# Attention B: projections of tiles 2 to 5 issued earlier, turned q and k in other banks, another order on VectorE and ScalarE

## The reference

```python
q = rope(x @ dequant(qw_q, scales_q)); k = rope(x @ dequant(qw_k, scales_k)); v = x @ dequant(qw_v, scales_v)
scores = where(causal, q @ k.T / sqrt(128), min)        # k, v shared by the 4 heads of a group
ctx = softmax(scores) @ v
out = ctx @ dequant(qw_o, scales_o)                      # dequant: (w - 8) * scale per 128 input rows
```

## Time and profile before

| | |
|---|---|
| median of 3 runs | 1567.97 us (1566.79 to 1569.36) |
| the profiled execution | 1571.05 us, span 1569.2 us |
| TensorE busy | 1469.0 us, 94% |
| VectorE busy | 1237.7 us, 79% |
| ScalarE busy | 868.9 us, 55% |
| GpSimd busy | 237.6 us, 15% |
| chain that ended last | PE 73%, DVE 14%, ACT 6%, DMA 3% |
| attention B's steps | 613.9 to about 1508 us |
| granted TensorE clock, mean | 0.972 |

### The profile page before, as it was taken

The page is one execution under the profiler, slowest core; times in us unless marked ns, Lnnn a source line. Parts: engine busy times, 40 slices in busy tenths (PEclk is TensorE's granted clock), DMA queues, the critical chain, the costliest instruction groups (busy, mean ns, idle before and its releaser), DMA issues.

```text
span 1569.2 us, 23528 instructions
## 1 busy us (share of the span) xinstructions
PE 1469.0 (94%) x7932; PEld 698.8 (45%) x7932; DVE 1237.7 (79%) x2583; ACT 868.9 (55%) x1468; POOL 237.6 (15%) x174
## 2 busy tenths in 40 slices
PE   5779999999999997899999999998999999999988
PEld 3412333333333354455555555554555555555534
DVE  4288888888886388787897887887887888878873
ACT  2205767676778324565665665664665665646630
POOL 2002000000000132221212212212212212211020
PEclk9957999999999998999999999999999999999989
DMA  3894000000000233566576575675684674653621
GB/s 97 150 143 134 1 1 0 0 0 0 0 0 11 64 94 98 105 140 144 121 137 139 120 150 127 129 147 120 128 160 111 141 145 110 134 96 67 115 54 54
DMA packets 352234, 144.64 MB, mean 92 GB/s; under 512 B 314680, under 2 KB 324408, under 8 KB 352128
## 3 DMA queue, kind: packets, MB, share of 16 engines
q1 hardware_dynamic: 352144, 143.48, 43.8%
HBM read 59.64 MB, written 6.19 MB: 42 GB/s over the span
## 4 chain that ended last, share of the span: by engine, by line
PE 73%; DVE 14%; ACT 6%; DMA 3%; issue 3%; SPq 0%; POOL 0%; DVEq 0%; ACTq 0%
PE ps L1433 9%; PE ps L1215 9%; PE ps L1435 9%; PE ps L1434 9%; PE ps L1268 7%; PE ps L1254 7%; PE ps L1395 4%; PE ps L1514 3%; PE ps L1516 3%; PE ps L1515 3%; ACT hl L680 2%; DVE hl L1038 2%; PE ps L1358 2%; DMA scratch<-pieces 2%; PE ps L1458 2%
## 5 line engine op out<-in xcount | busy, mean ns | idle before, releaser
L672 ACT ACTIVATE x<-ps,nmb,factor 128x128 f32<-128x128 f32 (+7 forms) x256 | 211.6, 832 | 290.9 <-DVE nmb L1023 290.9
L823 DVE TENSOR_REDUCE mx<-ps 128x1 f32<-128x512 f32 x512 | 326.4, 686 | 52.8 <-PE ps L1215 49.4
L581 ACT ACTIVATE proj<-ps 128x1024 f32<-128x1024 f32 x256 | 248.4, 1021 | 105.7 <-PE ps L1254 104.8
L1215 PE MATMUL ps<-ks,qs 96*128 (+1 forms) x512 | 200.1, 414 | 16.3 <-DVE mx L823 8.5
L1038 DVE SCALAR_TENSOR_TENSOR hl<-x,rden,hl 128x128 f16<-128x128 f32 (+7 forms) x256 | 208.3, 814 | 4.6 <-ACT hl L680 4.3
L680 ACT ACTIVATE hl<-x,rden 128x128 f16<-128x128 f32 (+7 forms) x256 | 184.1, 767 | 23.2 <-DVE rden L1034 22.5
L1021 DVE TENSOR_REDUCE nmr<-ps 128x1 f32<-128x128 f32 (+7 forms) x256 | 191.9, 750 | 0.0
L500 POOL TENSOR_TENSOR tmp<-tmp 128x640 f32<-128x640 f32 x64 | 98.4, 1538 | 532.1 <-DVE tmp L1017 532.1
L1433 PE MATMUL ps<-wh,xTh 128*128 128x256 f16 (+1 forms) x512 | 167.6, 327 | 0.0
L1434 PE MATMUL ps<-wl,xTh 128*128 128x256 f16 (+1 forms) x512 | 167.5, 327 | 0.0
L1435 PE MATMUL ps<-wh,xTl 128*128 128x256 f16 (+1 forms) x512 | 167.4, 327 | 0.0
(11 more groups left out here) (155 smaller groups left out, 2149.6 us busy)
## 6 DMA issues: line engine op xcount, KB each, us to landing
scale<-sp_n SPq DMA_DIRECT2D x32, 384.0 KB, 4.3
st<-in_L_attn_b_qw_q_dram SPq DMA_DIRECT2D x32, 256.0 KB, 2.8
st<-in_L_attn_b_qw_o_dram SPq DMA_DIRECT2D x32, 256.0 KB, 3.0
scale<-so_n SPq DMA_DIRECT2D x32, 256.0 KB, 3.6
qs<-scratch SPq DMA_DIRECT2D x24, 256.0 KB, 8.4
hlT<-hl SPq DMA_TRANSPOSE x256, 3.5
scratch<-pieces SPq DMA_DIRECT2D x5, 768.0 KB, 13.4
xnat<-attn_a_hidden_state_dram SPq DMA_DIRECT2D x8, 256.0 KB, 4.8
```

The lines of the kernel that those rows point to most:

```text
L581: nc.scalar.activation(pbuf[:, e % 4, :].rearrange("p (b n) -> p b n", b=2), ps[:, b:b + 2, :], ACT.Exp, scale=float(HD) ** -0.5).then_inc ...
L672: nc.scalar.activation(pr[:, h, 0:n], flat(2 * (h % 2), n), ACT.Exp, bias=nmb[:, h:h + 1], scale=factor[:, par, 0:1], accum_out=den[:, h:h ...
L823: nc.vector.tensor_reduce(mx[:, f, k // 2, k % 2:k % 2 + 1], ps[:, bank(k), :], AX.X, ALU.max).then_inc(s_mx, 1)
L1215: mm(ps[:, bank, :], qs[0:STACK, ds(g * R + h, 1), f * HALF + qt * P:f * HALF + (qt + 1) * P], ks[0:STACK, ds(g, 1), kh * HALF:(kh + 1) * ...
```

## The change

- `turned_banks`: the turned q and k of tiles 1 to 4 go to banks 1 and 3 in place of 6 and 7, on all engines that write or read them.
- TensorE: the projections of tiles 2 to 5 stand at the end of the steps of tiles 0 to 3, behind everything else, in place of behind the first scores of the steps of tiles 1 to 4. In the steps of tiles 1 to 3 `values` stands in front of `turn_b`.
- VectorE: in tile 0's step the previous tile's last low part stands in front of the first maximum; in the steps of tiles 1 to 4 the second maximum stands in front of the rotation; in the steps of tiles 0 to 4 the dequantisation stands behind `turned`.
- ScalarE: `high_part` stands behind the fourth exponential, in all steps.

```diff
--- before.py
+++ after.py
@@ -217,6 +217,10 @@
         def v_slot(t, par):
 
             return t if t > 1 else t + T * par
+
+        def turned_banks(t):
+
+            return (1, 3) if 1 <= t <= T // 2 else (6, 7)
 
         def k_slot(t, par):
 
@@ -642,10 +646,10 @@
 
             def turned(v, t, par):
                 act.wait_ge(s_qkT, v + 1)
-                nc.scalar.activation(qTh[:, t % 2].rearrange("p h n -> p (h n)"), ps[:, 6, :], ACT.Copy,
+                nc.scalar.activation(qTh[:, t % 2].rearrange("p h n -> p (h n)"), ps[:, turned_banks(t)[0], :], ACT.Copy,
                                      scale=HEADROOM / (XSCALE * WSCALE)).then_inc(s_qke, 1)
                 c = k_slot(t, par) * P
-                nc.scalar.activation(kTh[:, c:c + P], ps[:, 7, 0:P], ACT.Copy,
+                nc.scalar.activation(kTh[:, c:c + P], ps[:, turned_banks(t)[1], 0:P], ACT.Copy,
                                      scale=HEADROOM / (XSCALE * WSCALE)).then_inc(s_qke, 1)
 
             def context_high(g, t):
@@ -686,12 +690,12 @@
                     values(u + 1, par if t < T - 1 else 1 - par, t2)
                 high(0)
                 high(1)
-                if not last:
-                    high_part(g + 1, t, 1 - par)
                 if not end:
                     turned(u + 1, t2, par if t < T - 1 else 1 - par)
                 exponentials(2)
                 exponentials(3)
+                if not last:
+                    high_part(g + 1, t, 1 - par)
                 if exists(*before(g, t, 1)):
                     context_high(*before(g, t, 1))
                 high(2)
@@ -1041,11 +1045,11 @@
             def turned(v, t, par):
 
                 dve.wait_ge(s_qke, v * 2 + 2)
-                nc.vector.scalar_tensor_tensor(qTl[:, t % 2].rearrange("p h n -> p (h n)"), ps[:, 6, :],
+                nc.vector.scalar_tensor_tensor(qTl[:, t % 2].rearrange("p h n -> p (h n)"), ps[:, turned_banks(t)[0], :],
                                                HEADROOM / (XSCALE * WSCALE), qTh[:, t % 2].rearrange("p h n -> p (h n)"),
                                                ALU.mult, ALU.subtract).then_inc(s_ql, 1)
                 c = slice(k_slot(t, par) * P, (k_slot(t, par) + 1) * P)
-                nc.vector.scalar_tensor_tensor(kTl[:, c], ps[:, 7, 0:P], HEADROOM / (XSCALE * WSCALE), kTh[:, c],
+                nc.vector.scalar_tensor_tensor(kTl[:, c], ps[:, turned_banks(t)[1], 0:P], HEADROOM / (XSCALE * WSCALE), kTh[:, c],
                                                ALU.mult, ALU.subtract).then_inc(s_ql, 1)
 
             def add(v, t, par):
@@ -1073,17 +1077,23 @@
                 one, two = before(g, t, 1), before(g, t, 2)
                 if exists(*one):
                     low(u - 1, 2, (one[1] + 1) * P)
+                if exists(*one) and t == 0:
+                    low(u - 1, 3, S)
                 if t == 0:
                     dve.wait_ge(s_fcr, g + 1)
                 maximum(u, 0, n, par)
-                if exists(*one):
+                if exists(*one) and t > 0:
                     low(u - 1, 3, (one[1] + 1) * P)
-                if not last:
+                sooner = t <= T // 2
+                if sooner and t > 0:
+                    maximum(u, 1, n, par)
+                elif not last and t > 0:
                     dequantise(g + 1, t)
                 if not end:
                     rope_cos(u + 1, t2)
                     rope_sin(t2)
-                maximum(u, 1, n, par)
+                if not sooner or t == 0:
+                    maximum(u, 1, n, par)
                 invert(u, 0)
                 if not end:
                     values_low(u + 1, par if t < T - 1 else 1 - par, t2)
@@ -1094,6 +1104,8 @@
                     turned(u + 1, t2, par if t < T - 1 else 1 - par)
                 else:
                     final_statistics(0, 1)
+                if sooner and not last:
+                    dequantise(g + 1, t)
                 low(u, 1, n)
                 invert(u, 1)
                 if exists(*two):
@@ -1450,11 +1462,12 @@
                 project(v, t, 1, par)
                 project(v, t, 0, par).then_inc(s_pj, 1)
 
-            def turn_b(v):
+            def turn_b(v, t):
                 pe.wait_ge(s_rpa, v + 1)
                 pe.wait_ge(s_vl, v + 1)
                 for h in range(BH):
-                    dst = ps[:, 6, h * P:(h + 1) * P] if h < R else ps[:, 7, 0:P]
+                    q, k = turned_banks(t)
+                    dst = ps[:, q, h * P:(h + 1) * P] if h < R else ps[:, k, 0:P]
                     ins = nc.tensor.transpose(dst, rc1[:, h * P:(h + 1) * P], ident[:])
                 ins.then_inc(s_qkT, 1)
 
@@ -1524,7 +1537,7 @@
                 one, two = before(g, t, 1), before(g, t, 2)
                 pe.wait_ge(s_ql, u * 2 + 2)
                 keys(g, t, 0, par)
-                if not end:
+                if not end and (t == 0 or t > T // 2):
                     project_all(u + 1, *after(g, t), par if t < T - 1 else 1 - par)
                 keys(g, t, 1, par)
                 if exists(*two):
@@ -1533,14 +1546,18 @@
                 if exists(*two):
                     output_second(*two, par if t >= 2 else 1 - par)
                 keys(g, t, 3, par)
+                if 1 <= t < T // 2:
+                    values(*one, par)
                 if not end:
-                    turn_b(u + 1)
-                if exists(*one):
+                    turn_b(u + 1, after(g, t)[1])
+                if exists(*one) and not 1 <= t < T // 2:
                     values(*one, par if t >= 1 else 1 - par)
+                if t < T // 2:
+                    project_all(u + 2, g, t + 2, par)
 
             project_all(0, 0, 0, 0)
             tokens(2, 4, 5)
-            turn_b(0)
+            turn_b(0, 0)
             tokens(2, 6, 7)
             steps(step)
             output_first(G - 1, T - 2, (G - 1) % 2)
```

## The result

The changed kernel is slower by half a per cent: by 9.7 us by the medians, and by 8.0 by the ratio of the runs (interval 4.2 to 11.9). That is about half of the 18.0 us forecast.

What follows compares the result with a forecast made beforehand. TensorE, busy 94%, was taken as the bound, with VectorE's queue taking over the waits. 6 x 2.8 us per period, +0.3 for the last group and +0.9 for the first gave +18.0 on 1567.97: 1586.0 us, range 1566 to 1597.

Steps and rivals of the forecast that it cites:

- The waits for kTl: TensorE ahead of the first scores of tiles 2, 3 and 4: waits of 1.74, 1.17 and 0.50 us disappear.
- the third scores' waits for the first exponential: TensorE in tiles 2 to 4: new gaps of some 1 us, since only the first output half (1.3 us) covers.
- The low parts: VectorE's third-head low parts, tiles 1 to 3: held by GpSimd's low part of the weights for 0.4, 0.4 and 0.3 us.
- Tile 0's order: VectorE in tile 0's step: no gain; turning 0.85 us sooner, but the values still wait for their DMA.
- the walk: Tracing engine queues from 849.49 us over tiles 1 to 4: tile 5's scores start 2.4 us later, at 900.3.
- The hold of the inversion: VectorE behind the sines: the inversion falls into GpSimd's addition and is held, so VectorE stands still for 1.6 us.
- Rival (b): The inversion isn't held either: chain 0.2 to 0.4 us shorter per tile, +0.3 per period, 1570 us; chance 0.10.
- Tiles 4 and 5: kTl comes 0.3 us after tile 4's values; tile 5's second exponential comes 0.4 us after TensorE wants it.
- The first and the last group: Attention B's end groups: +0.9 us in the first, +0.3 in the last, which has no dequantisation or GpSimd low part.
- (a): No hold on the low parts and exponentials a little earlier: 1.3 us per period, about +9, 1577 us; chance 0.14.
- Rival (c): VectorE isn't the bound in tiles 2 to 4: faster, -1.5 us per period, 1556 us; chance 0.16.
- Rival (d): Two more VectorE collisions with GpSimd's low part, tiles 4 and 7: up to +1.6 us per period, 1597; chance 0.16.

Runs made afterwards that it cites:

- experiment 3: Changed kernel with the dequantisation of tiles 1 to 4 ahead of the low parts of the turned q and k: 1563.7 us, ratio 0.9963.
- experiment 6: Changed kernel with GpSimd's low part of weight chunks 1 to 3 cut to 2 of 768 columns from group 2 on: 1571.07 us.
- experiment 2: Kernel before with only tile 0's new VectorE order, and that tile's weights' high part behind the exponentials: 1573.38 us, ratio 1.0031.
- experiment 5: Changed kernel with the second maximum of tiles 1 to 4 behind the rotation again, one execution: 1594.64 us.
- before_again: Kernel before, unedited, profiled a second time for its granted clock: 1568.98 us.
- after_again: Changed kernel, unedited, profiled a second time for its granted clock: 1579.64 us.
- experiment 4: Changed kernel with the k and v half of tile 2's projection ahead of tile 7's values: 1561.85 us, ratio 0.9942.
- experiment 8: Changed kernel with both dequantisation of tiles 1 to 4 sooner and half of tile 2's projection ahead of tile 7's values: 1553.68 us, ratio 0.9888.
- experiment 9: Both kernels profiled again; also changed kernel with tile 0's old VectorE order and half of tile 2's projection ahead of tile 7's values: 1566.39 us, ratio 0.9982.
- Experiment 1: Changed kernel with VectorE's old order in tile 0's step: 1574.8 us, ratio 1.0038.

## Why the prediction was right or wrong

**Right: the side, and what takes over.** Slower, 1578.31 us, inside 1566 to 1597. The waits for kTl went and the third scores' waits for the first exponential came, 0.92, 0.97 and 1.01 us for a forecast of some 1 us; experiments 3 and 6 show that VectorE's queue sets them. The low parts were held by 0.4, 0.4 and 0.3 us, the values that the prediction took, and experiment 6 takes the hold away. Tile 0's order wins nothing: the values of tile 7 start 0.24 to 0.25 us behind their landing in both kernels (experiment 2), and the gap of 1.18 stands as 1.20 at the other end of the step.

**Wrong: the size, +18.0 us forecast, +9.7 measured by the medians and +9.8 in attention B between the profiled executions.** Two terms were mis-sized, one was put at nothing, the walk has a slip, and the terms of the first and the last group stay open.

*The hold of the inversion.* The step that failed is "The inversion of the first two sums, now straight behind the sines, falls into GpSimd's addition." The row was read rightly: in the earlier trace rows the inversion starts 1 us into the addition and is held, and experiment 5 shows it again. But a VectorE instruction follows its predecessor by 0.08 us less than its drawn end, and GpSimd starts 0.08 behind it. So the inversion comes first, by 0.17, and is done when GpSimd begins. The numbers for this stood in the walk itself, but the prediction weighed who starts first only for its last rival, and not here. The Trainium skill (SBUF — State Buffer, SBUF: two separate sides) says that of a VectorE and a GpSimd instruction that both need the shared pair of ports, whichever starts first has it for its whole length. By that rule, the trace agrees: 0.16 us at 855.93.

What this cost the forecast isn't 1.6 us per tile. Counted from the start of tile 7's values, GpSimd's addition in tile 1 ends at 14.32 us, as forecast. With the inversion went the 0.56 between the addition and the turning: in the earlier trace rows that was vl behind the held inversion. Now the turning starts 0.05 behind the addition, and waits 0.52 for a forecast of 1.03 in tile 1, and 0.73 for 1.2 in tile 4. VectorE's next round, from the end of that addition to the end of tile 2's, takes 11.3 us for a forecast of 11.8, because the turned halves come 0.5 us sooner. The two rounds behind it take 25.3 to 25.7 us for 25.8: there the time that the inversion gives back is spent in waiting for ScalarE (0.79 us ahead of qTl in tile 1), and partly in the addition holding the next low part (0.77 for 0.48 in tile 1), which I had not seen. Rival (b) had said so: 0.2 to 0.4 per tile and no more.

*Tiles 4 and 5.* With VectorE and GpSimd some 1.2 to 1.5 us earlier at tile 4's turning, kTl comes in time (0 for 0.3) and so does tile 5's second exponential (0 for 0.4). There is a slip of 0.4 beside it: the prediction's list of waits gives 2.0 us more (5.7 for 3.7) where its starts give 2.4, and it took the 2.4. Per period the waits grew by 0.9 us in place of 2.8: six periods, 5.4 for 16.8 (4.7 by the starts, without the low stretches).

*The first and the last group.* Forecast +0.9 and +0.3, measured -1.0 and -0.7. The clock is in both: with half a microsecond taken off for each at half clock, they come out as +1.3 and +0.3 in the first two profiles, as forecast, but as -0.2 and -0.6 in the second two, `before_again` and `after_again`. So these two terms stay open.

*The clock: forecast nothing, measured 6.8 us in four low stretches.* Net of the longer time at half clock that the kernel before has at the ends of attention B it is some 3.5 us of the 9.8, and by the mean clocks of all executions some 5 of 9.3. So a third to a half of the loss comes from something that the prediction didn't have, and the waits, forecast at 18.0 us, are worth some 4 to 6. The prediction took tile 0's step for unchanged because its idle time is nearly unchanged, 2.3 to 2.5 us before and 2.3 to 2.7 after. That the time came out at half of the forecast, and not at a quarter or a third, is luck: the clock made up for part of the waits that were too large. None of the rivals had it. That the low stretches cost is shown by their windows, and that half a projection between the turning and the values removes them by experiments 4, 8 and 9, in three kernels out of three. What brings them is not settled. Experiment 1 has the gaps of the kernel before in tile 0's step and three low stretches; experiment 2 has the kernel before's projections and one. All that the runs show is the place, from 650 to 1480 us always the start of tile 7's values, in the step with the most idle time, and that the kernel before escaped it in both profiles.

Of the rivals, (b), the inversion not held, named the right mechanism at 0.10 and gave +0.3 per period and 1570 for it. It took the held low parts away as well; with them left in, as they were, the prediction's own step from (a) to (b), 1.0 per period, would have given 2.8 - 1.0 = 1.8 per period, about 1580, still twice the waits that were measured. Rival (c), VectorE no bound, is refuted by experiment 3. Rival (d), two more collisions, didn't come. The ties that it speaks of are there, and VectorE wins them; in tile 4:

```profile
898.48 0.16 DVE L1035 TENSOR_SCALAR rden<-den 128x2 f32<-128x2 f32 x1
...
898.55 1.16 POOL L512 TENSOR_TENSOR wol<-st,woh 128x512 f16<-128x512 f32 x1 [3.95 <-ACT woh L606]
```

In tiles 4 to 7 of all seven groups, 28 times, the inversion starts 0.02 to 0.08 us ahead of GpSimd's low part and takes its plain 0.16 to 0.17.

## What to carry to other kernels

When a wait is moved off a chain, walk the queue of the engine that is then behind it once round, and ask of each stretch where that engine idles: an instruction with slack (here the dequantisation) belongs there and not behind the work that others wait for. That move and 1.3 us of work in front of a DMA landing turned a loss of 0.5% into a gain of 1.1%. For two engines that share a port, write down both start times before charging a hold: 0.17 us decided whether VectorE stood for 1.6. A hold costs a chain only the part that the engine wouldn't have waited anyway: here 0.5 us in a round, not 1.6. And idle time that is only moved isn't free where it costs clock: in experiment 2 the same idle time in another order cost 4 us of it. What makes the clock fall there isn't known, so compare the mean granted clock of ten or so executions before trusting a sum of waits.

## What the runs showed of the hardware

- A scalar_tensor_tensor with two SBUF inputs (the low part) is held too, until about 0.2 us before GpSimd's drawn end: 0.88 us for 0.48 at 863.05, and 0.48 again when GpSimd's instruction is 0.20 us long. Others run on inside the same addition in the changed kernel: the reciprocal (856.13, 0.17 us), vl, which reads PSUM (856.36, 0.29), a maximum (856.57, 0.41) and nmb, a tensor_scalar of 128x1 (857.02, 0.21).
- TensorE can start 0.05 us behind GpSimd's drawn end (857.64 and 857.69).
- The granted clock fell to half for 3.4 us behind a cluster of three gaps, 2.3 to 2.7 us in all and the longest of 1.2 to 1.5, in three or four of seven periods of the changed kernel, and in none of two profiles of the kernel before with 2.3 to 2.5. Ten runs of one kernel (experiment 2) then spread over 16 us, where twenty of the kernel before spread over 7.
